# A graph network kernel: order of the first pass's loads, ScalarE's start, and who makes the one-hot tiles of GIN1

## The reference

```python
agg = segment_sum(x[src], dst)                       # L0: GIN, one layer
h = relu((x + agg) @ W1 + b1) @ W2 + b2; h = relu(batch_norm(h))
agg = segment_sum(x[src], dst)                       # L1: GIN with 256 hidden units
h = relu((x + agg) @ W1 + b1); h = relu(h @ W2 + b2) @ W3 + b3
for l in range(3):                                   # L2: messages and a GRU cell
    m = relu(cat(h[src], h[dst], e) @ W1[l] + b1[l]) @ W2[l] + b2[l]
    h = gru(segment_sum(m, dst), h)
for l in range(2):                                   # L3: attention (GAT)
    h = segment_softmax(...) weighted sum of (h @ W)[src]
x = layernorm(x + network(x))                        # after each of the four
```

## Time and profile before

| | before |
|---|---|
| median of 3 runs | 3148.66 us |
| the profiled execution's own time | 3150.42 us |
| its span, first to last instruction | 3148.3 us |
| PE busy | 2591.5 us (82%) |
| DVE busy | 2291.5 us (73%) |
| POOL busy | 2238.1 us (71%) |
| ACT busy | 1510.4 us (48%) |
| pass 0, first gather to last gather issued | 5.4 to 408.3 us |
| pass 1, first gather to last gather issued | 485.5 to 848.9 us |

### The profile page before, as it was taken

How to read it: one execution, slowest core, us unless ns; L and a number is a source line. 1 busy time by engine, 2 the same in 40 slices (tenths; PEclk the granted TensorE clock), 3 DMA queues, 4 the chain that set the end, 5 groups by cost and what they waited for, 6 DMA issues and landing times. The chain is left out here.

```text
span 3148.3 us, 72955 instructions
## 1 busy us (share of the span) xinstructions
PE 2591.5 (82%) x27587; PEld 2368.0 (75%) x27587; DVE 2291.5 (73%) x6950; ACT 1510.4 (48%) x2670; POOL 2238.1 (71%) x2227
## 2 busy tenths in 40 slices
PE   6899758999398999579999579996789994699971
PEld 6799637999267999549999369996479994599871
DVE  5898736876325999857999559999458875578776
ACT  3655321111037777357887268884524443244442
POOL 5677746777637777677777677777477776777774
PEclk9899858999688999779999789998789996699985
DMA  5888817998317999649999379996178883588861
GB/s 172 320 325 289 255 39 251 370 339 290 110 30 270 339 337 338 197 132 310 340 341 319 85 242 337 340 339 219 31 226 270 279 259 111 145 262 272 257 192 41
DMA packets 331283, 757.12 MB, mean 240 GB/s; under 512 B 114547, under 2 KB 163389, under 8 KB 284252
## 3 DMA queue, kind: packets, MB, share of 16 engines
q1 hardware_dynamic: 252408, 669.39, 60.0%
q0 software_dynamic: 70912, 71.66, 11.0%
q10 hardware_dynamic: 7780, 14.10, 1.2%
HBM read 559.21 MB, written 195.71 MB: 240 GB/s over the span
## 5 line engine op out<-in xcount | busy, mean ns | idle before, releaser
L1587 PE MATMUL ps<-big 128*128 128x192 bf16 (+1 forms) x22854 | 2067.8, 248 | 0.4 <-issue 0.3
L692 POOL DMA_INDIRECT ringG<-tab,src_i x1638 | 1634.4, 998 | 538.2 <-issue 488.9
L1587 PEld LDWEIGHTS ps<-big 128*128 128x128 bf16 x22854 | 1927.4, 98 | 61.4 <-issue 15.4
L1063 DVE SCALAR_TENSOR_TENSOR ringG<-ringG,same 128x64 f32<-128x64 f32 x2075 | 585.2, 282 | 145.8 <-DMA ringG<-tab,src_i 77.8
L777 ACT COPY big<-ps 128x384 f32<-128x384 f32 (+1 forms) x468 | 187.1, 455 | 387.6 <-PE ps L1587 387.0
L692 POOL DMA_INDIRECT ringG<-in_x,src_i x273 | 286.9, 1051 | 116.3 <-issue 82.3
L1063 DVE SCALAR_TENSOR_TENSOR edge_side<-edge_side,same 128x64 f32<-128x64 f32 x1245 | 348.6, 280 | 10.1
L804 ACT ACTIVATE big<-big,ones 128x1408 bf16<-128x1408 bf16 x234 | 333.9, 1458 | 2.5
L1173 DVE SCALAR_TENSOR_TENSOR ringG<-ringG,expo 128x65 f32<-128x65 f32 x830 | 239.8, 289 | 100.5 <-ACT ringG L823 22.1
L1032 DVE TENSOR_SCALAR big<-big,node_f 128x1408 bf16<-128x1408 int16 x441 | 257.8, 610 | 73.6 <-PE ps L1587 39.7
L1032 DVE TENSOR_SCALAR big<-src_hot_b,node_f 128x1408 bf16<-128x1408 int16 x430 | 251.4, 610 | 38.7 <-PE ps L1587 32.5
(11 more groups left out here) (276 smaller groups left out, 2217.8 us busy)
## 6 DMA issues: line engine op xcount, KB each, us to landing
big<-kept SPq DMA_DIRECT2D x234, 1056.0 KB
big<-kept SPq DMA_DIRECT2D x78, 1408.0 KB
sums<-ringG SPq DMA_DIRECT2D x260, 256.0 KB
kept<-big SPq DMA_DIRECT2D x39, 1056.0 KB
edge_side<-q_at_start SPq DMA_DIRECT2D x156, 256.0 KB
sums_w<-ringG SPq DMA_DIRECT2D x104, 264.0 KB
ringG<-tab,src_i POOLq DMA_INDIRECT x1638
edge_side<-ef_mix SPq DMA_DIRECT2D x117, 160.0 KB
```

Source lines behind the costliest of these rows:

```text
L692: return pool.indirect_dma_start(out=out_ap, out_offset=None, in_=table, in_offset=bass.IndirectOffsetOnAxis(ap=index, axis=0))
L1063: return v.scalar_tensor_tensor(now, before if u == 0 else source[:, (u - 1) * D:u * D], same[:, c:c + 1], now, ALU.mult, ALU.add)
L1587: mm = pe.matmul(ps[:, b, 0:256 + n] if wide else ps[:, b, to:to + n], hot[t][:, u * P:(u + 1) * P], opener[:, 0:256 + n] if wide else spl ...
```

## The change

1. In SP's queue the load of `xN` moves ahead of the six loads of `dst`.
2. The sources of unit 2 of pass 0 are loaded right after the stores of unit 0. The 61 weight loads leave their place behind those stores. They are issued in eight parts, one behind each of the trips 0 to 7.
3. ACT's first tile of pass 0 waits for `numbered` (node numbers negated by DVE), not for `split_ready`. The tile of the last piece still waits for `split_ready`, since its buffer is scratch of the split.
4. Pass 1 lends ACT six tiles (2, 1, 1 and 2 of the four pieces). DVE makes six instead of twelve; 13 are fed as before. In ACT's order the copies of unit i+1 keep their place in group 1 of a trip in pass 1. The wait for `pq` is for passes 2 and up alone.

```diff
-PASSES = ([Pass(0, HOT, lent=(1, 1, 1, 1)), Pass(1, HOT, fed=KEPT)]
+PASSES = ([Pass(0, HOT, lent=(1, 1, 1, 1)), Pass(1, HOT, fed=KEPT, lent=(2, 1, 1, 2))]
...
+WEIGHT_TRIPS = 8
...
                 sp.dma_start(hot_stage[n][:], a[f"hot_src{n}"]).then_inc(hot_src_in, 16)
+            sp.dma_start(xN[:], x_d.rearrange("(t p) d -> p t d", p=P)).then_inc(x_in, 16)
...
-            sp.dma_start(xN[:], x_d.rearrange("(t p) d -> p t d", p=P)).then_inc(x_in, 16)
...
-                if i == 0:
+                if i == 0 and k:
                     load_sources(k, 2)
...
-            for dst, s in weight_loads:
-                sp.dma_start(dst, s).then_inc(weights_in, 16)
+            load_sources(0, 2)
             for q in range(len(TILES)):
                 keep_piece(1, q)
             for i in range(FIRST_AT + 1):
                 trip(0, i)
+                for dst, s in weight_loads[i:len(weight_loads):WEIGHT_TRIPS] if i < WEIGHT_TRIPS else []:
+                    sp.dma_start(dst, s).then_inc(weights_in, 16)
...
                     if q == 0 and k == 0:
+                        act.wait_ge(numbered, 1)
+                    elif k == 0 and q == len(TILES) - 1:
                         act.wait_ge(split_ready, 1)
                     elif q == 0:
                         act.wait_ge(bank_done, BANKS_BEFORE[k])
-                        act.wait_ge(*done(f"pq{k - 2}", NC - 1))
+                        if k >= 2:
+                            act.wait_ge(*done(f"pq{k - 2}", NC - 1))
...
-                        if j == (GROUPS - 1 if lent else 1) and i + 1 < TRIPS:
+                        if j == (GROUPS - 1 if lent and k != 1 else 1) and i + 1 < TRIPS:
...
-            link(v.tensor_scalar(node_minus[:], node_f[:], -1.0, None, ALU.mult))
+            v.tensor_scalar(node_minus[:], node_f[:], -1.0, None, ALU.mult).then_inc(numbered, 1)
```

More of the change, by code:

```diff
@@ L361, in build @@
         vchain = sem("vchain")
-        split_ready = sem("split_ready")
+        split_ready, numbered = sem("split_ready"), sem("numbered")
         src_hot_in = [sem(f"src_hot_in{s}") for s in range(2)]
```

## The result

The changed kernel takes 3110.69 us (median of 4 runs, 3107.25 to 3112.32), the kernel before in the same session 3148.23 (3147.72 to 3150.0). The ratio is 0.9882, with a 95% interval of 0.9871 to 0.9894. That is 37.5 us less. The forecast was 3114.

A forecast was written before the change was run, and what follows sets the result against it. POOL was taken to pace pass 0, held by one stop on unit 2's sources. Gains of 31.6 (pass 0) and 3.2 (GIN1), 34.8 us together, against 3148.66 gave 3114 us; range 3104 to 3122.

The forecast's parts named there:

- What bounds the kernel: Pass 0: POOL paces it and has one stop of 33.3 us, behind DVE's 29.07 us wait for unit 2's sources.
- The sources and xN: Start of pass 0: source wait goes, xN brings 4.1 us; 43rd gather at 62.4, not 94.03, gaining 31.6 us.
- ACT's early tiles at nothing: Start of pass 0: ACT starts some 7 us earlier, but PE's first matmul waited for DVE's tile; counted 0.
- Pass 0 keeps it: Rest of pass 0: POOL keeps the 31.6 us gained at its 43rd gather, though DVE gains only 29.6.
- 30 to 33 us earlier: Sign at the end of pass 0: the last gather comes this much earlier (376).
- (a): Rival, pass 0: xN no use, or DVE carries the end; gain 27.5 to 29.6, total 3117 us; 15 in 100.
- The weights at nothing: SP's queue, pass 0: weights cost some 5 us behind a trip, but what stands behind them has slack; counted 0.
- GIN1: Pass 1: six fewer DVE tiles a trip shorten POOL's gathers, 0.30 us a trip over 11 trips, 3.2 us.
- (b): Rival, pass 1: tiles held POOL up more, so the edit gives the whole 14.3 us, total 3103; 7 in 100.
- (c): Rival, pass 1: sources wait for ACT's tiles, feeds bunch; up to 1 us a trip lost, 3119 to 3130; 11 in 100.
- (d): Rival, pass 1: PE waits for ACT's tiles every unit, counting past 28.0 us a unit; slower, 3187; 3 in 100.
- (e): Rival, pass 0: early source load lands past 52 behind unit 0's stores, stop partly stays; 3120 to 3145; 2 in 100.

The follow-up runs named there:

- The sources alone: Kernel before with unit 2's sources loaded right behind unit 0's stores and the weights behind trips 0 to 7; xN, ACT's wait and GIN1 unchanged: 3121.84 us.
- the one with xN first: Changed kernel with the load of xN issued as the very first, ahead of the indices and the hot sources: 3107.42 us.
- xN alone: Kernel before with xN loaded ahead of dst and ACT's first tiles not behind the split; sources, weights and GIN1 unchanged: 3144.89 us.

## Why the prediction was right

**What bounds the kernel: right.** The one long stop of POOL was what held pass 0 up, and removing it moved the time.

**The sources and xN: right.** Split, first matmul and 43rd gather came at 7.80, 19.28 and 62.23, against 7.9, 19.3 and 62.4. The sources alone gave what the sum said: POOL went on at 68.31 where the prediction had 66.5, and the difference is xN's late issue in that run. PE became the late one.

**ACT's early tiles at nothing: right as far as seen.** In the changed kernel ACT's tiles were ready first, and PE's first matmul waited for DVE. The edit was not run apart from xN's.

**Pass 0 keeps it: off by 2 us.** 31.8 us were gained at the 43rd gather and 29.6 at the last one (33.3 and 30.2 between the two repeated profiles). So 2 to 3 us are lost on the way. The prediction let POOL keep all of 31.6, and its sign "30 to 33 us earlier" at the last gather was missed by 0.4 us. Its rival (a) named 29.6, but for another reason, that DVE would carry the end. That didn't happen: at the last group DVE waits 4.89 us for its gathers, as before (4.95):

```profile
380.16 2.53 DVE L1068 SCALAR_TENSOR_TENSOR ringG<-ringG,same 128x64 f32<-128x64 f32 x8 [4.89 <-DMA ringG<-in_x,src_i]
```

**The weights at nothing: perhaps mis-sized.** This is one likely place of the 2 us. POOL needs 316.5 to 318.8 us from the 43rd to the last gather in seven of the eight kernels that load weights within the trips, and 312.7 to 315.5 in the six that load them ahead. The eighth, the one with xN first, needed 315.2. The gathers that POOL begins between 95 and 376 us had a mean of 1045 ns before (209 of them) and have 1063 now (206). POOL has no stop there, so it is not a late store, against which the prediction held its ring of 8 groups. The gathers themselves are longer. Whether that is by the weights' transfers or because pass 0's work now lies differently was not separated. Two kernels speak against the weights as the whole cause. In the eighth trip of the pass the mean gather takes 1.082 us in the changed kernel and 1.032 before. With xN first it takes 1.014, though the weights are loaded within the trips, and with xN alone 1.069, though they are not.

**GIN1: the mechanism right, the size in part luck.** The passes with twelve tile instructions on DVE took 358.8 to 360.1 us (six profiles, without the first), those with six 356.8 to 358.4 (five). The mean of the one lies 2 us above that of the other, where 3.2 was forecast. The 5.1 us between the two first profiles is mostly the long pass 1 of the first one.

The forecast's 0.028 us a gather came from two windows of that one profile, and it does not stand. One gather more or less in a window of 44 moves a mean by 0.02, as much as the difference itself. Counted by the gathers begun in the 58 us before the tiles end, and by those begun after, the first profile gives 1.012 and 0.984, but the repeated one 0.986 and 0.983. In the two windows of the changed kernel above, the difference has the other sign. That 3.2 came near was luck.

What the tiles do is seen in the single gathers. They are of two kinds. In pass 1 of the kernel before, run again, 204 of 273 take at most 1.00 us, nearly all of them 0.94. The other 69 hold nearly all of the excess. These are two neighbours, of which the second runs beside two tiles:

```profile
501.16 0.94 POOL L692 DMA_INDIRECT ringG<-tab,src_i  x1 [0.30 <-issue]
502.41 1.14 POOL L692 DMA_INDIRECT ringG<-tab,src_i  x1 [0.30 <-issue]
```

| tile instructions of DVE in a trip of pass 1 | gathers over 1.00 us | what all gathers take above 0.944 us each |
|---|---|---|
| twelve, kernel before and its edits (six profiles) | 65 to 78 | 18.1 to 22.8 us |
| twelve, changed kernel with tiles made twice | 64 | 19.5 us |
| six (five profiles) | 45 to 54 | 16.1 to 17.8 us |
| four (eight tiles on ACT) | 40 | 14.4 us |

The counts do not overlap. The gathers that became fewer are those that run beside a tile. Of them 37 to 53 are long in the six profiles of the first line, 31 with the tiles made twice, 16 to 25 with six and 16 with four. Those that are long without a tile beside them stay at 24 to 33. A gather during which DVE does nothing never takes more than 0.95 us in these kernels. So fewer tiles do shorten the pass, and the 359.7 us of the kernel with four on DVE are its one stop.

The rival (b), 14.3 us, is out: DVE's twelve instructions put back cost 2 to 3 us (360.1), not 14. By the rule of the Trainium skill ("SBUF — State Buffer", "Who interferes with whom"), that a tensor_scalar in a two-port mode shuts GpSimd out for the whole instruction, it would have been up to 40 us, an estimate from 66 instructions of 0.61. The trace disagrees with it for these tiles in size, by more than a factor of ten. It agrees in that a tile can hold POOL up: the prediction looked at the one gather at 494.69, which took 0.94, and 42 of the 116 that overlap a tile in the repeated profile are longer than 1.00. The trace doesn't name the mode in which the tiles run. Why one gather beside a tile is held up and the next is not stays open.

**The missing term.** Passes 2 to 4 got 5 us shorter. The prediction followed the tiles and the queues and not the values that the waits compare, though the diff moves them: `LENT_BEFORE` depends on the list of passes. With its 5 us the forecast would have been 3109. The 2 to 3 us lost in pass 0 go the other way, so part of how near the forecast of 3114 came is that two misses stand against each other.

**Rivals.** (a) had a number near what pass 0 kept, but not the reason. (c) didn't come: POOL has no stop in pass 1 of the changed kernel. (d) came only when provoked: at 29.25 us of ACT's work a unit pass 1 grows and the gain is gone. Its threshold of 28.0 us fits that, but no kernel between eight and ten tiles was run. (e) didn't come: in trip 0 DVE no longer waits for the sources.

The sum, against the profile of before: 29.6 for pass 0, 5.1 for pass 1, 4.5 for passes 2 to 4, 2.1 for 5 and 6, 1.8 for the rest, 43.1 of 43.2 together. Against the repeated profiles of both kernels, 44.1. The medians say 37.5 and 42.2. What lies between is scatter of a few microseconds from run to run. The pass lengths outside the change's reach vary by 1 to 3 us between profiles too.

## What to carry to other kernels

Where a load stands behind others in a queue, look for all that stands behind the same block. Here moving the sources without the weights gained a third, and the rest came only when the stores on which the next tiles also waited were freed too. Once the engine that paces a pass no longer stops, an earlier start of its neighbours is worth nothing, and what lengthens each of its own instructions counts. Where such a lengthening is a matter of few collisions, a mean over two short windows of one profile doesn't size it: take the whole pass, and a second profile. And when a diff changes a list from which wait values are computed, compare the values in all passes, not only in the one that is edited.

## What the runs showed of the hardware

- A gather (one indirect DMA of 128 rows issued by POOL) costs POOL 0.94 us and 0.30 of issue. During 51 gathers of pass 1 of the kernel before, run again, DVE does nothing, and none of them takes more than 0.95. Of the rest a part takes 0.1 to 0.7 us more, and the first and third of the pass 2.53 and 2.33 us. In that pass 69 of 273 are over 1.00 us, and the excess of all is 19 us.
- The load issued right behind xN's holds SP's queue for 2.65 to 3.36 us in all 14 profiles, whichever load it is: the unit's sources, `dst`, or the source indices (2.79). Each of the latter two takes 0.41 to 0.43 us in the profiles where it stands elsewhere near the start. Small loads of a few bytes per partition (`beside_i`) cost SP between 0.25 and 2.78 us each, and that moves the first microseconds from kernel to kernel: xN is issued at 5.77 before and at 7.33 with the sources alone, behind the same loads.
- Two ScalarE instructions of 1.46 us by their records follow each other in 1.36 us when ScalarE is full. So a sum of record durations overstates a full engine by 7%.
- Making the two values equal that TensorE waits for at each piece, far off the path, made 819 gathers of POOL's (273 in each of three passes) 5 us shorter in sum (1061.2 against 1066.2 us with their issue).
